# Splitting half of the experts' weights one layer earlier, and taking the two products of an expert tile in turns

## The chip, the cores and the metric

The program runs on one core of a Trainium2 chip. The metric is device microseconds of one execution, median of several runs; the times here are of that one core, and the profile is of one further execution of the same program. PE is TensorE (PEld its weight loads), DVE VectorE, ACT ScalarE, POOL GpSimd, SP the sync engine that only issues DMAs.

## What is computed

A two-layer network on 4096 tokens of width 256 (128 sequences of 32), with a context of 257 rows for each sequence. Layer 0 is softmax cross-attention, a state space block and a quantized feed-forward block; layer 1 is cut out here, with what the change touches:

```python
x = x + _L1_xattn_ref(_layernorm(x, axis=-1), ctx_1024, ctx_1024, L1_xattn_Wq, L1_xattn_Wk, L1_xattn_Wv, L1_xattn_Wo)  # sigmoid
x = x + _L1_attn_ref(_layernorm(x, axis=-1), L1_attn_w_qkv, L1_attn_w_proj, L1_attn_b_proj)                            # softmax
x = x + _L1_ffn_ref(_layernorm(x, axis=-1), L1_ffn_switch_w, L1_ffn_switch_b, L1_ffn_w1, L1_ffn_b1, L1_ffn_w2, L1_ffn_b2)
...
logits = t @ switch_w + switch_b
route_prob = jax.nn.softmax(logits, axis=-1)
route_prob_max = jnp.max(route_prob, axis=-1)
routes = jnp.argmax(route_prob, axis=-1)
for e in range(n_experts):                     # 8 experts, 256 -> 1024 -> 256
    h = jax.nn.gelu(t @ w1[e] + b1[e])
    y = h @ w2[e] + b2[e]
    mask = (routes == e)[:, None]
    out = jnp.where(mask, y, out)
out = out * route_prob_max[:, None]
```

Each token goes through one expert of eight.

## The kernel before

Every float32 factor is kept as two float16 halves, a high and a low one, and a product of two factors is three products on PE (high by high, high by low, low by high). The work is written out by hand: each engine has its own list of instructions in a fixed order, and counts in semaphores tie the lists together. An engine that waits holds up everything behind it in its list. Each layer is a block with a barrier at its end.

**Experts' weights.** There are 16 pieces (two per expert) of 128 by 2048 numbers, split into halves in the tile `ea_w` (`Ahead.W`). Splitting a piece is: SP loads it, ACT writes the high half (`hi_w`, a scaled copy), DVE or POOL writes the low half (`lo_w`, the staged number minus the high half). Pieces 0 to 7 are split in self-attention, a quarter of a piece in each of its 32 steps: `hi_w` (L2458) stands last in ACT's step and `lo_w` (L2569) last in DVE's, just ahead of `add_max` of the step after the next. Pieces 8 to 15 are split in `sort_tokens`, which finds each token's expert: DVE takes four of them in the loop over 32 token tiles, POOL four behind it. The space of pieces 8 to 15 is lent to tiles of self-attention (`lent`) until then.

**Sigmoid cross-attention** (`x_` names, L934) runs over 128 sequences in 32 groups of four. In a sequence PE computes scores, keys of the sequence after the next, one of three small jobs for the next group (`turn`), `attend` of the sequence before the last, and values of the next one. DVE's list for the second sequence of a group (j = 1) ends with `lo_q`; behind it come, for j = 2, `extract` (L1398, `x_oT`) and `lo_v` (L1391, `x_vl`). PE's `attend` (L1219) waits for that `extract`, and PE's next `values` (L1105, `x_psV`) for that `lo_v`. POOL's `spread` (L1066) starts when `lo_q` is done.

**Self-attention** (`a_` names, L2131) has 32 steps of 128 tokens. DVE's step is: `add_max` of the next step, `lo_pT` (L2550), a few more, `extract` (L2559), `lo_ob`, `lo_q` or `lo_v`, `count`, `lo_w`. PE's `attend` waits for `lo_pT`, ACT's and DVE's `extract` for `attend`.

**Expert tiles** (`e1t_` names, L2899). 39 tiles of up to 128 tokens of one expert. For a tile, PE transposes the normalised rows (L2950), then `hidden`: 8 blocks k of four products with 256, 128, 256, 128 columns (L2966, L2967), then `outputs` of the tile before: 8 pairs with 512 and 256 columns (L2978, L2979). The expert's number is only known at run time, so the address of a weight comes from a register: an instruction that works it out stands ahead of each hidden product and of each pair of output products, and `value_load` reads the number behind the transposes. Between the tiles this chain runs:

```python
act.wait_ge(h_mm, s * 2 + (half + 1))             # take_low, L3016: PE's last hidden product of tile s
dve.wait_ge(low_taken, s * 2 + (half + 1))        # add_bias, L3115
dve.wait_ge(row_in[c], i * 16 + 16)               # normalise(s + 2), L3099, behind add_bias in DVE's list
pe.wait_ge(xn_done, s + 1)                        # transpose(s), L2950, ahead of value_load and hidden in PE's list
```

so `transpose(s + 2)`, which PE's list has at the start of tile s + 1, waits for the last hidden product of tile s by way of ACT and DVE.

Of the kernel before, what the change touches and what calls it, by code (L numbers as in the profile page):

```python
# [18 lines left out]
P = 128  # L19
D = 256  # L20
# [913 lines left out]
def sigmoid_attention(nc, d, xres, con, norm):  # L934
# [4 lines left out]
    with ExitStack() as ctx:  # L939
# [10 lines left out]
        ctxp = parts("ctx", [P, GB, C, LAST], 2)  # L950
# [4 lines left out]
        vxr = [sb(f"vxr{n}", [64, GB, D], F16) for n in range(2)]  # L955
        vxm = [sb(f"vxm{n}", [64, GB, D], F16) for n in range(2)]
# [56 lines left out]

        @block.sync
        def _(sync):
# [29 lines left out]
            run(sync, body)  # L1045

# [207 lines left out]
        def _(act):  # L1254
# [50 lines left out]

            def hi_ob(i, gp):
# [17 lines left out]
            def body(i):  # L1324
                for c in range(8):
# [15 lines left out]
            hi_ob(LASTI, 1)  # L1341

        @block.vector
        def _(dve):
# [36 lines left out]
            def lo_k(i, c):  # L1381
# [3 lines left out]
                dve.tensor_tensor(flat(K[c % 4][1]), psK[:], flat(K[c % 4][0]), ALU.subtract).then_inc(k_lo, 1)  # L1385

# [39 lines left out]
            def body(i):  # L1426
                for c in range(8):
# [19 lines left out]
            residual(LASTI, 1)  # L1447

# [682 lines left out]
def self_attention(nc, d, xres, con, norm, ahead):  # L2131
# [10 lines left out]
    with ExitStack() as ctx:  # L2142
# [10 lines left out]
        late = ahead.W[:, AHEAD:].rearrange("p n h f -> p (n h f)")  # L2153
        free = [0]

        def lent(dims, turns, axes):

            size, pairs = math.prod(dims.values()), []
            for _ in range(turns):
                pairs.append(tuple(late[:, free[0] + n * size:free[0] + (n + 1) * size].rearrange(axes, **dims) for n in range(2)))  # L2160
                free[0] += 2 * size
            return pairs
# [24 lines left out]
        w_in, w_hi, w_lo = sem("w_in"), sem("w_hi"), sem("w_lo")  # L2187
        stage = sb("stage", [P, PIECE], F32)
# [216 lines left out]
        def _(act):  # L2405
# [72 lines left out]
            def body(i):  # L2478
                for c in range(2 * U):
# [16 lines left out]
                    hi_w(i, c)  # L2496
# [3 lines left out]
        def _(dve):  # L2500
# [68 lines left out]
            def lo_w(i, c):  # L2569
                g = i * 2 * U + c  # L2570
                dve.wait_ge(w_hi, g + 1)
                dve.scalar_tensor_tensor(ahead.W[:, g // 4, 1, quarter(g)], stage[:, quarter(g)], WS,
                                         ahead.W[:, g // 4, 0, quarter(g)], ALU.mult, ALU.subtract).then_inc(w_lo, 1)

# [20 lines left out]
            def body(i):  # L2595
                for c in range(2 * U):
# [19 lines left out]
                    lo_w(i, c)  # L2616
# [7 lines left out]

class Ahead:
# [3 lines left out]
    def __init__(self, nc, sp, d):  # L2629
        self.W = sp.sb("w", [P, 16, 2, PIECE], F16)  # L2630
# [637 lines left out]
```

## Time and profile before

| | |
|---|---|
| median of 3 runs | 2903.12 us (2901.89 to 2906.99) |
| the profiled execution | 2901.02 us |
| its span | 2899.2 us, mean granted clock 0.928 |
| PE busy | 2486.8 us (86%) |
| DVE busy | 2180.6 us (75%) |
| ACT busy | 1935.3 us (67%) |
| POOL busy | 1614.3 us (56%) |

The span is from the first to the last instruction; the execution's own time has 1.8 us around it. The busy time is a sum over stages with different limits. By the starts of their first instructions the stages that the change touches are the sigmoid cross-attention (about 1480 to 2106 us), self-attention (to 2494), the sort (to 2591) and the expert tiles (to the end). The granted clock is PE's, as a share of 2.4 GHz.

### The profile page before, as it was taken

Reading aid. Unit: us, or ns where it says so; the run is one execution under the profiler, and the core shown is the slowest. Engines: PE = TensorE matmul, PEld = TensorE weight load, DVE = VectorE, ACT = ScalarE, POOL = GpSimd, SP = SyncE. Lnnn points to the kernel's source line nnn. Section 1 sums busy time; section 2 is a strip of 40 time slices with the busy share of each in tenths; the row PEclk is TensorE's granted clock in tenths of the full one; section 3 lists DMA queues with packets and bytes.
Section 4 is the critical chain, followed back from the end, with each engine's and each line's share of the span. In section 5 each row is a group of like instructions: output and inputs, shape, how many; then the busy total and the mean of one; then the engine's idle time right before and its main releaser. Section 6 shows DMA issues by size and latency. Waiting matters only on the chain. (4 is left out here: it accounts for less than half of the span.)

```text
span 2899.2 us, 97754 instructions
## 1 busy us (share of the span) xinstructions
PE 2486.8 (86%) x38790; PEld 1920.0 (66%) x38790; DVE 2180.6 (75%) x4939; ACT 1935.3 (67%) x4320; POOL 1614.3 (56%) x1709
## 2 busy tenths in 40 slices
PE   3999999999928999976969999999947777639997
PEld 2777777777715777753548888888736666526665
DVE  4899999999947999974367777777658888456665
ACT  2788888888838999943447777777735555335554
POOL 3776777777534555520056766666436566435554
PEclk9999999999958999997989999999969889559999
DMA  5222222222100000000022221222011111221110
GB/s 155 64 75 70 70 71 83 70 70 71 31 15 1 1 1 1 1 15 17 1 86 68 68 63 57 68 68 68 19 36 35 37 43 44 84 65 36 38 38 29
DMA packets 123292, 140.20 MB, mean 48 GB/s; under 512 B 17184, under 2 KB 115264, under 8 KB 120672
## 3 DMA queue, kind: packets, MB, share of 16 engines
q1 hardware_dynamic: 114992, 123.60, 14.2%
q0 software_dynamic: 3744, 10.31, 1.2%
q8 instruction: 316, 5.18, 0.8%
q14 instruction: 128, 1.05, 0.1%
q10 hardware_dynamic: 4112, 0.07, 0.1%
HBM read 123.78 MB, written 10.16 MB: 46 GB/s over the span
## 5 line engine op out<-in xcount | busy, mean ns | idle before, releaser
L2081 DVE TENSOR_TENSOR_SCAN m_s<-m_a,m_psBx 128x2048 f32<-128x2048 f32 x64 | 282.7, 4417 | 21.6 <-PE m_psBx L1856 18.8
L1377 DVE SCALAR_TENSOR_TENSOR x_pTl<-x_psS,x_pTh 128x1024 f16<-128x1024 f32 x128 | 156.7, 1224 | 174.1 <-ACT x_pTh L1285 174.1
L676 ACT ACTIVATE x_prob<-x_prob,x_low 128x257 f32<-128x257 f32 x512 | 254.4, 513 | 5.2 <-DVE x_low L802 3.5
L1867 PE MATMUL m_psS<-m_s,all_ident 128*128 128x256 f32 x1024 | 237.3, 385 | 0.9 <-DVE m_s L2081 0.9
L1867 PEld LDWEIGHTS m_psS<-m_s,all_ident 128*128 128x128 f32 x1024 | 190.2, 191 | 42.8 <-issue 18.2
L802 DVE CUSTOM_DVE_ANT_0 x_prob<-x_psS,x_masked,x_prob 128x256 f32<-128x256 f32 x512 | 216.1, 477 | 1.6 <-PE x_psS L558 1.4
L1988 ACT ACTIVATE m_a<-m_dt,m_rate 128x248 f32<-128x248 f32 x512 | 205.8, 489 | 5.0 <-DVE m_s L2081 4.6
L691 ACT ACTIVATE x_kh<-x_psK,x_bk 128x256 f16<-128x256 f32 x256 | 107.3, 470 | 131.7 <-PE x_psK L442 131.7
L817 DVE SCALAR_TENSOR_TENSOR x_pTl<-x_psT,x_pTh 128x512 f16<-128x512 f32 x256 | 163.4, 679 | 0.5 <-ACT x_pTh L684 0.5
L2966 PE MATMUL e1t_psH<-e1t_xnp,ea_w 128*128 128x256 f16 x624 | 159.8, 284 | 2.3 <-issue 0.5
L1066 POOL TENSOR_TENSOR x_qbdh<-x_qh,all_mask4h 128x1024 f16<-128x1024 f16 x32 | 60.6, 1893 | 181.6 <-DVE x_ql L1358 181.6
L2290 PE MATMUL a_psO<-ea_w 128*64 128x128 f16 x1536 | 98.5, 264 | 71.8 <-DVE ea_w L2550 71.8
L2235 POOL TENSOR_TENSOR ea_w<-ea_w,all_mask4h 128x1024 f16<-128x1024 f16 x64 | 121.3, 1899 | 61.5 <-DVE ea_w L2511 61.5
L1058 POOL TENSOR_TENSOR x_ctxl<-x_ctx,x_ctxh 128x512 f16<-128x512 f32 x128 | 149.4, 1167 | 10.6
L1298 ACT ACTIVATE x_vh<-x_psV 128x512 f16<-128x512 f32 x128 | 76.4, 597 | 116.8 <-PE x_psV L1105 116.8
L347 POOL TENSOR_TENSOR x_ctxl<-x_ctx,x_ctxh 128x512 f16<-128x512 f32 x128 | 148.4, 1159 | 10.7
L442 PE MATMUL x_psK<-x_ctxh,x_wkh 128*128 128x256 f16 x512 | 141.2, 276 | 6.2 <-POOL x_ctxl L347 5.0
L2290 PEld LDWEIGHTS a_psO<-ea_w 128*64 128x64 f16 x1536 | 92.6, 138 | 80.8 <-DVE ea_w L2550 80.8
L1279 ACT ACTIVATE x_psS<-x_psS 128x1024 f32<-128x1024 f32 x128 | 129.0, 1008 | 24.3 <-PE x_psS L1199 24.3
L1105 PE MATMUL x_psK<-x_ctxh,x_wkh 128*128 128x256 f16 x512 | 141.2, 276 | 3.9 <-POOL x_ctxl L1058 3.6
L3060 POOL TENSOR_TENSOR e1t_hidl<-e1t_g,e1t_hidh 128x512 f16<-128x512 f32 x78 | 93.0, 1192 | 92.3 <-ACT e1t_hidh L3032 89.6
L3115 DVE SCALAR_TENSOR_TENSOR all_xres<-e1t_psH,e1t_bias,all_xres 128x128 f32<-128x128 f32 x312 | 87.9, 344 | 74.2 <-ACT all_xres L3016 37.4
(552 smaller groups left out, 10071.3 us busy)
## 6 DMA issues: line engine op xcount, KB each, us to landing
x_ctx<-in_ctxT SPq DMA_DIRECT2D x64, 1024.0 KB, 6.1
x_mraw<-in_mask SPq DMA_DIRECT2D x128, 128.5 KB, 2.8
a_stage<-in_L_ffn_w SPq DMA_DIRECT2D x8, 1024.0 KB, 5.0
e1r_stage<-in_L_ffn_w SPq DMA_DIRECT2D x8, 1024.0 KB, 5.1
all_xres<-in_x SPq DMA_DIRECT2D x1, 4096.0 KB, 14.5
x_vxr<-x_vx SPq DMA_DIRECT2D x128, 32.0 KB, 3.6
e_x<-all_xres SPq DMA_DIRECT2D x32, 128.0 KB, 2.0
x_vxr<-x_vx SPq DMA_DIRECT2D x96, 8.0 KB, 2.3
```

The lines of the kernel that those rows point to most:

```text
L347: pool.tensor_tensor(lo[:, j], src, hi[:, j], ALU.subtract).then_inc(ctx_split, 1)
L442: last = pe.matmul(out, a, b, start=m == 0, stop=m == len(prods) - 1)
L676: act.activation(prob[c % 4][:, h, :], prob[c % 4][:, h, :], ACT.Exp, bias=low[c % 4][:, h:h + 1], scale=-1.0, accum_out=sm[c % 2][:, h:h ...
L802: dve.tensor_tensor_reduce(prob[c % 4][:, h, 0:LAST], psS[:, to:to + LAST], masked[gp][:, j, 0:LAST], -SC, prob[c % 4][:, h, LAST:S2], ALU ...
L817: dve.scalar_tensor_tensor(turned(pT[c % 2][1], r), strip_of(psT, r), PS, turned(pT[c % 2][0], r), ALU.mult, ALU.subtract).then_inc(pt_lo, 1)
L1058: pool.tensor_tensor(lo[:, j], src, hi[:, j], ALU.subtract).then_inc(ctx_split, 1)
L1377: dve.scalar_tensor_tensor(pT[c % 4][1][:].rearrange("p r k n -> p (r k n)"), psS[c % 2][:], PS, pT[c % 4][0][:].rearrange("p r k n -> p ( ...
L1867: last = pe.matmul(psS[:, h * ST:(h + 1) * ST], con["ident"][:], S[h][:, :, m, :], start=m == 0, stop=m == NS - 1)
L1988: last = act.activation(A[h][:, :, m, 1:T], dt[c % 2][:, h, :].rearrange("p (b t) -> p b t", t=T)[:, :, 1:T], ACT.Exp, scale=rate[:, h, m: ...
L2081: dve.tensor_tensor_scan(rows(S), rows(A), psBx[:], 0.0, ALU.mult, ALU.add).then_inc(scan_done, 1)
L2290: last = pe.matmul(out, a, b, start=m == 0, stop=m == len(prods) - 1)
L2966: pe.matmul(at, wh, x[:, :, cc, :], start=cc == 0, stop=False)
```

## The change

1. The loads, `hi_w` and `lo_w` of pieces 0 to 7 move from self-attention into the sigmoid cross-attention: one quarter piece per group of four sequences, `hi_w` behind ACT's list for j = 3, `lo_w` behind DVE's list for j = 1, two staging buffers of a quarter instead of one of a whole piece. To make room, larger tiles of that layer (`ctx`, `vxr`, `vxm`, `qbd`, K, V, `pT`) live in the space of pieces 8 to 15 (`Lent`), so the weights' tile exists from that layer on and is called `ew_w`.
2. In `sort_tokens` the transposed tiles have three buffers instead of two, PE transposes two tiles ahead, DVE writes three low halves (pieces 0, 2 and 4 of the eight) and POOL five: two in the loop over tiles and three behind it. The last two high halves on ACT stand ahead of the copy that waits for DVE's `tile_ready`.
3. In the expert tiles, PE takes the 8 blocks of `hidden` of tile s and the 8 pairs of `outputs` of tile s - 2 in turns; outputs lie one tile further back, and `hid` has three buffers.

```diff
 # sigmoid_attention
+            def load_w(q):
+                wait(sync, w_lo, q - 1)
+                sync.dma_start(stage[q % 2][:], d["L1_ffn_w"][q // 4][:, quarter(q)]).then_inc(w_in[q % 2], 16)
 ...
                     load_vx(i, gp)
+                    if i * 2 + gp:
+                        load_w(i * 2 + gp - 1)
 ...
+            def hi_w(q):
+                act.wait_ge(w_in[q % 2], (q // 2 + 1) * 16)
+                act.activation(experts_w[:, q // 4, 0, quarter(q)], stage[q % 2][:], ACT.Copy, scale=WS).then_inc(w_hi, 1)
 ...
+                    if j == 3 and i * 2 + c // 4:
+                        hi_w(i * 2 + c // 4 - 1)
 ...
+            def lo_w(q):
+                dve.wait_ge(w_hi, q + 1)
+                dve.scalar_tensor_tensor(experts_w[:, q // 4, 1, quarter(q)], stage[q % 2][:], WS,
+                                         experts_w[:, q // 4, 0, quarter(q)], ALU.mult, ALU.subtract).then_inc(w_lo, 1)
 ...
+                    if j == 1 and i * 2 + c // 4 > 1:
+                        lo_w(i * 2 + c // 4 - 2)
             run(dve, body)
 ...
             residual(LASTI, 1)
+            lo_w(NT - 2)
+            lo_w(NT - 1)
 # self_attention
-                    hi_w(i, c)
 ...
                     if exists(i, c, -1):
                         count(i, c)
-                    lo_w(i, c)
             run(dve, body)
 # sort_tokens
-    LATE, BY_POOL = 16 - AHEAD, 4
+    LATE = 16 - AHEAD
+    BY_DVE = {0: 1, 2: 2, 4: 3}
+    BY_POOL = {1: 1, 3: 2, 5: 3, 6: 4, 7: 5}
 ...
             transpose(0)
+            transpose(1)
             for t in range(NT):
-                if t + 1 < NT:
-                    transpose(t + 1)
+                if t + 2 < NT:
+                    transpose(t + 2)
                 logits(t)
 ...
-            scale_w(LATE - BY_POOL)
+            for k in (6, 7):
+                scale_w(k)
+                hi_w(k)
             act.wait_ge(tile_ready, 1)
             act.activation(named[:, :, 1, :], oh_tile, ACT.Copy, scale=row[:]).then_inc(row_ready, 1)
-            for k in range(LATE - BY_POOL + 1, LATE):
-                scale_w(k)
 ...
-            for k in range(LATE - BY_POOL, LATE):
-                hi, lo = halves(k)
-                pool.wait_ge(w_hi, k + 1)
-                pool.tensor_tensor(lo, stage[k % 2][:], hi, ALU.subtract).then_inc(w_lo_pool, 1)
-            pool.wait_ge(w_lo_pool, BY_POOL)
+                if t in (13, 23):
+                    lo_w((t - 8) // 5)
+            for k in (5, 6, 7):
+                lo_w(k)
+            pool.wait_ge(w_lo_pool, len(BY_POOL))
 # expert_tiles, PE
-                    if exists(i, c, 1):
-                        transpose(*at(i, c, 1))
-                        e[s + 1] = expert(pe, *at(i, c, 1))
-                    if exists(i, c, 0):
-                        hidden(i, c, e[s])
-                    if exists(i, c, -1):
-                        outputs(*at(i, c, -1), e.pop(s - 1))
-            run(pe, body)
+            for s in range(SLOTS + 2):
+                if s + 1 < SLOTS:
+                    transpose(s + 1)
+                    e[s + 1] = expert(pe, s + 1)
+                for k in range(FC):
+                    if s < SLOTS:
+                        hidden(s, e[s], k)
+                    if s >= 2:
+                        outputs(s - 2, e[s - 2], k)
+                e.pop(s - 2, None)
 # expert_tiles, DVE: the order is kept, and finish lies one tile further back
-                    if exists(i, c, -1):
-                        finish(*at(i, c, -1))
+                if s >= 2:
+                    finish(s - 2)
```

PE's list in the middle of the expert tiles, before: the last hidden product of a tile, the eight pairs of output products (the first and the last shown), the transposes, the expert's number (TENSOR_LOAD), and the first product of the next tile. ISA rows are the register instructions.

```order
L2967 MATMUL e1t_psH<-e1t_xnp,ea_w 128x128
L2978 ISA
L2978 MATMUL e1t_psY<-ea_w,e1t_hidh 128x512
L2979 MATMUL e1t_psY<-ea_w,e1t_hidl 128x256
...
L2950 MATMUL e1t_psX<-all_ident,e1t_xn 128x128 x2
L2941 TENSOR_LOAD e_owner
L2941 ISA x2
L2966 ISA
L2966 MATMUL e1t_psH<-e1t_xnp,ea_w 128x256
```

The same place now (the names are the same but for `ew_w`; lines are those of the changed kernel): the last block of hidden products, one pair of output products, the transposes.

```order
L2977 MATMUL e1t_psH<-e1t_xnp,ew_w 128x256
L2978 ISA
L2978 MATMUL e1t_psH<-e1t_xnp,ew_w 128x128
L2987 ISA
L2987 MATMUL e1t_psY<-ew_w,e1t_hidh 128x512
L2988 MATMUL e1t_psY<-ew_w,e1t_hidl 128x256
L2965 MATMUL e1t_psX<-all_ident,e1t_xn 128x128 x2
L2954 TENSOR_LOAD e_owner
L2954 ISA x2
L2977 ISA
L2977 MATMUL e1t_psH<-e1t_xnp,ew_w 128x256
```

Between the last hidden product and the transposes there were eight pairs of output products; now there is one, and the other seven stand among the hidden products.

DVE's list in the sigmoid cross-attention, from j = 1 into j = 2, before:

```order
L1385 TENSOR_TENSOR x_kl<-x_psK,x_kh 128x512
L1358 TENSOR_TENSOR x_ql<-x_psM,x_qh 128x256
L1361 TENSOR_TENSOR x_qx<-x_psM,x_kx 128x128 x2
L1398 SCALAR_TENSOR_TENSOR x_oT<-x_psO,all_mask,x_oT 128x2x64
L1391 TENSOR_TENSOR x_vl<-x_psV,x_vh 128x512
L1377 SCALAR_TENSOR_TENSOR x_pTl<-x_psS,x_pTh 128x1024
```

And now, with tiles of the layer inside `ew_w`:

```order
L1405 TENSOR_TENSOR ew_w<-x_psK,ew_w 128x512
L1378 TENSOR_TENSOR x_ql<-x_psM,x_qh 128x256
L1381 TENSOR_TENSOR x_qx<-x_psM,x_kx 128x128 x2
L1409 SCALAR_TENSOR_TENSOR ew_w<-x_stage,ew_w 128x512
L1423 SCALAR_TENSOR_TENSOR x_oT<-x_psO,all_mask,x_oT 128x2x64
L1416 TENSOR_TENSOR ew_w<-x_psV,ew_w 128x512
L1397 SCALAR_TENSOR_TENSOR ew_w<-x_psS,ew_w 128x1024
```

`lo_w` (L1409) has come between the last work of j = 1 and `extract` and `lo_v` of j = 2.

## Rows read from the trace of the kernel before

**Rows 1.** Windows: us, busy of PE, PEld, DVE, ACT, POOL, granted clock, DMA

```profile
1480.00:2095.00 615.00, 611.02 (x13114) 498.28 (x13115) 428.86 (x692) 457.74 (x728) 410.73 (x351) 0.99 0.21 61
2165.00:2485.00 320.00, 240.11 (x3776) 202.92 (x3775) 258.69 (x479) 178.84 (x327) 191.48 (x149) 0.89 0.11 37
2605.00:2880.00 275.00, 271.92 (x1883) 180.19 (x1884) 168.41 (x484) 153.79 (x303) 161.32 (x148) 1.00 0.12 36
```

**Rows 2.** Chain that ended last: output products of tiles 2 and 35

```profile
2624.06 0.39 PE e1t_psY L2978
...
2866.64 0.39 PE e1t_psY L2978
```

**Rows 3.** Timeline, PE, tiles 4 and 5: start, duration, what

```profile
2631.18 0.23 PE L2967 MATMUL e1t_psH<-e1t_xnp,ea_w 128*128 128x128 f16 x1
2631.43 0.39 PE L2978 MATMUL e1t_psY<-ea_w,e1t_hidh 128*128 x1
...
2634.04 0.38 PE L2950 MATMUL e1t_psX<-all_ident,e1t_xn 128*128 128x128 f32 x2
2634.45 0.28 PE L2966 MATMUL e1t_psH<-e1t_xnp,ea_w 128*128 128x256 f16 x1
2634.57 0.23 PE L2967 MATMUL e1t_psH<-e1t_xnp,ea_w 128*128 128x128 f16 x1
```

**Rows 4.** Timeline, ACT and DVE, end of the same tile 4

```profile
2631.45 0.60 ACT L3016 ACTIVATE all_xres<-e1t_psH 128x512 f32<-128x512 f32 x1 [1.59 <-PE e1t_psH L2967]
...
2633.12 0.41 DVE L3099 TENSOR_SCALAR e1t_xn<-e1t_row 128x256 f32<-128x256 f32 x1
```

**Rows 5.** Timeline of PE, tiles 0 and 1, then a window there

```profile
2600.87 0.22 PE L2967 MATMUL e1t_psH<-e1t_xnp,ea_w 128*128 128x128 f16 x1
2600.93 0.27 PE L2966 MATMUL e1t_psH<-e1t_xnp,ea_w 128*128 128x256 f16 x1
2601.03 0.22 PE L2967 MATMUL e1t_psH<-e1t_xnp,ea_w 128*128 128x128 f16 x1
...
2604.19 0.69 PE L2950 MATMUL e1t_psX<-all_ident,e1t_xn 128*128 128x128 f32 x2 [2.17 <-DVE e1t_xn L3099]
...
2604.10:2607.40 3.30, 3.03 (x17) 2.16 (x18) 0.46 (x2) 2.75 (x6) 2.04 (x2) 0.50 0.00 0
```

**Rows 6.** Self-attention, DVE and POOL: timeline, then the line, then its group

```profile
2318.33 1.89 POOL L2235 TENSOR_TENSOR ea_w<-ea_w,all_mask4h 128x1024 f16<-128x1024 f16 x1 [3.34 <-DVE ea_w L2511]
...
2318.50 2.27 DVE L2572 SCALAR_TENSOR_TENSOR ea_w<-a_stage,ea_w 128x512 f16<-128x512 f32 x1
2320.69 0.41 DVE L2533 SCALAR_TENSOR_TENSOR a_prob<-a_psS,all_phi 128x256 f32<-128x256 f32 x1
...
L2572 DVE SCALAR_TENSOR_TENSOR ea_w<-a_stage,ea_w x32: 666/676/2271, 2171.0 to 2492.3; 128x512 f16<-128x512 f32 x32
...
L2572 DVE SCALAR_TENSOR_TENSOR ea_w<-a_stage,ea_w 128x512 f16<-128x512 f32 x32 | 42.3, 1321 | 0.0
```

**Rows 7.** Sigmoid cross-attention, timeline of POOL, DVE and PE in one group

```profile
1806.29 1.89 POOL L1066 TENSOR_TENSOR x_qbdh<-x_qh,all_mask4h 128x1024 f16<-128x1024 f16 x1 [5.94 <-DVE x_ql L1358]
...
1806.53 0.34 DVE L1398 SCALAR_TENSOR_TENSOR x_oT<-x_psO,all_mask,x_oT 128x128 f32<-128x128 f32 x1
1806.78 0.68 DVE L1391 TENSOR_TENSOR x_vl<-x_psV,x_vh 128x512 f16<-128x512 f32 x1
...
1808.78 0.21 PE L1219 MATMUL x_psO<-x_pTh,x_vh 128*32 128x64 f16 x4
...
1809.42 0.28 PE L1105 MATMUL x_psV<-x_wvh,x_ctxh 128*128 128x256 f16 x1
```

**Rows 8.** Timeline of DVE and POOL, end of the sort

```profile
2582.10 0.18 DVE L2896 CAST e_token<-e1r_own 128x39 uint32<-128x39 f32 x1
...
2586.05 4.05 POOL L2799 TENSOR_TENSOR ea_w<-e1r_stage,ea_w 128x2048 f16<-128x2048 f32 x1 [5.05 <-ACT ea_w L2767]
2591.67 1.19 POOL L3066 DMA_INDIRECT e1t_row<-e_x,e_token  x1 [1.57 <-SPq L2904]
```

More of the change, by code:

```diff
@@ L1341, in _ @@
             hi_ob(LASTI, 1)
+            hi_w(NT - 1)
         @block.vector
@@ L2151, in parts @@
             return [(sb(f"{name}h{n}", shape, F16), sb(f"{name}l{n}", shape, F16)) for n in range(turns)]
[L2153 to L2162, printed above, removed]
+        lent = Lent(ahead.W)
         xn = sb("xn", [P, 2, D], F32)
@@ L2622, with __init__, __call__ @@
 PIECE, AHEAD = C * 8 * P, 8
+class Lent:
+    def __init__(self, experts_w):
+        self.late, self.used = experts_w[:, AHEAD:].rearrange("p n h f -> p (n h f)"), 0
+    def __call__(self, dims, turns, axes, rows=P):
+        size, pairs = math.prod(dims.values()), []
+        for _ in range(turns):
+            pairs.append([self.late[0:rows, self.used + n * size:self.used + (n + 1) * size].rearrange(axes, **dims) for n in range(2)])
+            self.used += 2 * size
+        return pairs
 class Ahead:
-    def __init__(self, nc, sp, d):
-        self.W = sp.sb("w", [P, 16, 2, PIECE], F16)
+    def __init__(self, nc, sp, d, experts_w):
+        self.W = experts_w
         self.x_dram = nc.dram_tensor("e1_x", (TOK + P, D + 4), F32, kind="Internal").ap()
@@ L2756, in _ @@
         def _(act):
-            def hi_w(k):
-                hi, _ = halves(k)
-                act.wait_ge(w_in[k % 2], (k // 2 + 1) * 16)
-                act.activation(hi, stage[k % 2][:], ACT.Copy, scale=WS).then_inc(w_hi, 1)
             def scale_w(k):
@@ L3050, in _ @@
-            run(act, body)
+                    wait(act, y_mm, s - 2)
+                act.activation(hid[s % 3][0][:, four(half), :], g[s % 2][:, four(half), :], ACT.Copy).then_inc(hid_hi, 1)
+            hi_xn(0)
+            take_bias(0)
+            for s in range(SLOTS):
+                if s + 1 < SLOTS:
+                    hi_xn(s + 1)
+                take_low(s, 0)
+                take_low(s, 1)
+                for half in range(2):
+                    gelu(s, half)
+                    hi_hid(s, half)
+                if s + 1 < SLOTS:
+                    take_bias(s + 1)
@@ L3089, in _, with gather, lo_hid @@
-            run(pool, body)
+            def gather(s):
+                wait(pool, o_done, s - U + 1)
+                pool.indirect_dma_start(row[s % U][:], None, x_dram, bass.IndirectOffsetOnAxis(ap=token[:, s:s + 1], axis=0))\
+                    .then_inc(row_in[s % U], 16)
+            def lo_hid(s, half):
+                pool.wait_ge(hid_hi, s * 2 + (half + 1))
+                if half == 0:
+                    wait(pool, y_mm, s - 2)
+                pool.tensor_tensor(hid[s % 3][1][:, four(half), :], g[s % 2][:, four(half), :], hid[s % 3][0][:, four(half), :],
+                                   ALU.subtract).then_inc(hid_lo, 1)
@@ new lines, in scatter @@
+            def scatter(s):
+                pool.wait_ge(o_done, s + 1)
+                wait(pool, put[(s - 1) % U], ((s - 1) // U + 1) * 16)
+                pool.indirect_dma_start(out, bass.IndirectOffsetOnAxis(ap=token[:, s:s + 1], axis=0), o[s % 4], None)\
+                    .then_inc(put[s % U], 16)
+            for s in range(EARLY):
+                gather(s)
+            for s in range(SLOTS + 2):
+                if s + EARLY < SLOTS:
+                    gather(s + EARLY)
+                if s < SLOTS:
+                    lo_hid(s, 0)
+                    lo_hid(s, 1)
+                if s >= 2:
+                    scatter(s - 2)
```

329 lines of the change are left out of this document (129 added, 200 removed).

## The prediction, made before the changed kernel ran

> **What bounds the kernel now.** I read the stages first, each for the wait that ends last in it. In the sigmoid cross-attention PE is busy 611 of 615 us and DVE 429: PE sets the pace, and only a delay of PE costs [rows 1]. In self-attention PE is busy 240 of 320 us, DVE 259, and the granted clock is 0.89: no engine is full, a loop through several engines is the limit [rows 1]. Its closed part is DVE's `lo_pT`, PE's `attend`, ACT's and DVE's `extract`, the rest of DVE's step, `lo_w`, `add_max`, and `lo_pT` again, so DVE time just ahead of `add_max` is on the path. In the expert tiles PE is busy 272 of 275 us at clock 1.00 [rows 1], which looks like a PE bound. It is not one. The output products of tiles 2 and 35 start at 2624.06 and 2866.64 us, so a tile takes 242.58 / 33 = 7.35 us [rows 2]. Inside it, the last hidden product of tile 4 starts at 2631.18 and the first of tile 5 at 2634.45, 3.27 us later, with the eight pairs of output products and the transposes between them [rows 3]. The same distance without any output products stands between tiles 0 and 1: the chain's transposes start at 2604.19 after 2.17 us of idle PE, released by DVE's normalising [rows 5]. In tile 4 that chain shows as ACT at 2631.45 and DVE's normalising at 2633.12 to 2633.53, while the transposes are held by the output products to 2634.04 [rows 3, 4]. So the 3.27 us are the chain PE, ACT, DVE, transposes, reading the expert's number, and the outputs (2631.43 to 2634.04, 2.6 us) lie in its shadow and are free. The other 7.35 - 3.27 = 4.08 us are 31 steps from one hidden product to the next, 0.13 us each, whether 256 or 128 columns (0.12 in the rows) [rows 3]. Where products had queued up while the array was slow, they go 0.06 and 0.10 us apart [rows 5]; so 0.13 us is the time of the instruction stream with its address instructions, and PE does buffer issued products.
>
> **Expert tiles: the sum.** In turns, a block is five address instructions, 5 x 0.13 = 0.65 us of issue, and at the array two times (0.10 + 0.06) plus a pair of outputs. Eight pairs take 2.6 us, so one takes 0.33, and the array needs 0.65 us [rows 3, 5]. Since PE buffers, a block takes the larger, 0.66 us; without buffering 4 x 0.13 + 0.33 = 0.85. From the first to the last hidden product of a tile that is 7 x 0.66 + 3 x 0.13 = 5.0 us, with 0.1 for the first block, where nothing is queued yet. The chain behind it is untouched by the edit: the same waits, and DVE still normalises tile s + 2 only behind the biases of tile s. So a tile takes 3.27 + 5.1 = 8.37 us. Only the last pair of outputs (0.33 us) is left in the shadow of the chain. Tiles 2 to 37 have both products and the chain, 36 x (8.37 - 7.35) = +37 us at full clock.
>
> Then the clock. PE now idles about 3.27 - 0.33 - 0.13 - 0.4 = 2.4 us in every tile, some 1.9 of it in one piece. The only tile that had such a gap, 2.17 us, was followed by a stretch at 0.50, 2604.1 to 2607.4 us [rows 5], that is 1.2 GHz. Self-attention, with PE three quarters busy and its idle time in one piece per step too, is granted 0.89 [rows 1]. In the new body a block is bound by the array as much as by issue, so a stretch of 3.3 us at half level does 3.3 / 1.31 = 2.5 blocks instead of 5 and costs 1.65 us. Never gives 8.37 us, in every tile 10.0. I take three tiles in four, 9.6 us: 36 x 2.25 = **+81 us**, bounds +37 and +96.
>
> The Trainium skill ("TensorE: Matmul & The Clock Gate", section "Why this matters for your kernels") asks only that PE not idle longer than what is idle here in one piece. By that rule the clock stays up and the stage costs +37. The row of tile 1 speaks against it.
>
> **Self-attention: -50 us.** The 32 `lo_w` leave DVE. They take 42.3 us, median 0.676, up to 2.271 [rows 6]. The long ones start while POOL's `spread` runs: 2318.50 against 2318.33 to 2320.22, and `add_max` follows at 2320.69, 2.19 us after [rows 6]. A short one holds the next up by 0.68 - 0.09 = 0.59 us. (42.3 - 32 x 0.676) / (2.27 - 0.676) = 13 are long: 13 x 2.19 + 19 x 0.59 = 39.7 us, all ahead of `add_max`, thus on the loop. What is late next is `attend`, which still waits for `lo_pT`: PE has 320 - 240 = 80 us of idle time, 2.5 us a step, so even 2.19 fits. `hi_w` on ACT is covered by ACT's waits (busy 179 of 320 us) and is taken at nothing, 0.5 us a step at most if not. Denser PE work also gives clock back: at 0.89, 22% of 320 us are at half level, 70 us; half the speed in the third or so of a step in which `attend` sets the pace is 12 us; I take 10. Bounds -36 (some of it kept by POOL) and -56.
>
> **Sigmoid cross-attention: +14 us.** 32 `hi_w` and `lo_w` arrive. ACT has 157 us free and PE does not wait for what is behind `hi_w`. `lo_w` is another matter: it stands right behind `lo_q`, which is what starts POOL's `spread`, 1806.29 to 1808.18. It would start at about 1806.53, be held to 1808.2 and end at 1808.75 [rows 7]. Behind it `extract` (now 1806.53, 0.34 us) would end at 1809.0 and `lo_v` (now 1806.78, 0.68 us) at 1809.65. PE's `attend` at 1808.78 waits for the one, `values` at 1809.42 for the other [rows 7]: both about 0.3 us late, and 0.1 more for `lo_k` behind them. 0.4 x 31 groups = 12.4 us, and the two last `lo_w` behind the layer's last `residual` add 1.3. Bounds: 0, since the slack is known to 0.3 us only, and 2.2 us a group, 68, if all of it reached PE.
>
> The Trainium skill ("SBUF — State Buffer", section "Who interferes with whom") says the port pair shared by VectorE and GpSimd is an exclusive lock for a whole instruction. Rows 6 agree for `lo_w`, 2.27 us against 0.68. If POOL kept the pair through both instructions of `spread`, each `lo_w` would be held 1.9 us more, and the layer would come near the upper bound.
>
> **Sort: -8 us.** The token numbers are ready at 2582.3, but POOL's last low half runs from 2586.05 to 2590.1 and the first gather starts at 2591.67 [rows 8]. Now the last high halves are ahead of the copy that waits for DVE, and POOL is through with 6 and 7 before 2570. The 7.8 us go. One POOL low half (4.05 us) moves into DVE's serial part and two into the loop, while the ones that overlapped DVE's end leave: I take these as even, bounds -18 and 0.
>
> **Sum**, against the profiled execution: 2901.0 + 81 - 50 + 14 - 8 = 2938 us. The profiled execution is 2.1 us below the median of the runs shown, less than I can tell; I leave it at 2938.
>
> **Rivals.**
> 1. The clock stays up in the tiles: +37 instead of +81, 2894 us, faster by 0.3%. For it: the clock is 1.00 in all tiles with a gap under a microsecond. Against it: tile 1. The step decides at 3 half-level stretches in 10 tiles. Chance 0.17.
> 2. `lo_w` in the cross-attention reaches PE in full: 68 instead of 14, 2992 us. For it: PE has no slack there. Against it: rows 7 leave 1.9 of 2.2 us before PE asks. Chance 0.07.
> 3. The chain is hidden after all, and PE runs at 8 x 0.66 + 0.4 = 5.7 us a tile: 36 x (5.7 - 7.35) = -59, 2798 us. For it: products that don't wait are ready while PE waits. Against it: PE's list is taken in order, and the transposes stand ahead of all of them. Chance 0.04.
> 4. The forecast, 0.72: its own range is 2912 to 2965 (the bounds of the clock in the tiles, and some 10 us for the other stages).
>
> **How the numbers follow.** 0.2%, about what a measurement of this kernel can tell, is 5.8 us. Of the forecast's 0.72 I give 0.70 to slower, rival 2 adds 0.07, rival 1 splits into 0.03 slower, 0.04 same and 0.10 faster, rival 3 is faster. Slower 0.79, same 0.06, faster 0.15. The range leaves out rivals 2 and 3 and takes in most of 1: 2892 to 2966.
>
> **What would show it.** Right: in the tiles the transposes start 2.4 us after the last hidden product, with PE idle; a tile takes over 8.3 us; stretches at 0.50 in most; the step of self-attention falls from 10.3 to about 8.8 us; `lo_w` in the cross-attention lasts about 2.2 us, and a group grows by 0.4. Wrong: a granted clock of 1.00 through the tiles, blocks of 0.85 us, or a tile below 7.35 us.

## The result, and the profile of the changed kernel

The changed kernel takes 2947.41 us (2945.67 to 2949.07, 4 runs) where the kernel before took 2905.05 in the same runs: ratio 1.0147, 95% interval 1.0129 to 1.0164: slower by 1.5%. The forecast was 2938, its range 2892 to 2966. The profiled execution has a span of 2944.2 us against 2899.2. By stage these 45.0 us are as follows. The stages are cut at PE's first product of the cross-attention, the end of DVE's last instruction there and in self-attention, and the start of POOL's first gather:

| stage | before | changed | difference | forecast |
|---|---|---|---|---|
| all ahead of the cross-attention | 1474.9 | 1472.2 | -2.6 | 0 |
| sigmoid cross-attention | 631.4 | 647.2 | +15.8 | +14 |
| self-attention (with its opening) | 388.3 | 340.1 | -48.1 | -50 |
| sort, to the first gather | 97.2 | 81.8 | -15.4 | -8 |
| expert tiles | 307.5 | 402.8 | +95.3 | +81 |

The -2.6 us lies in layers that the change doesn't touch.

**Windows** of the changed kernel (us, busy of PE, PEld, DVE, ACT, POOL, granted clock, DMA), the same three stages as in [rows 1], then two stretches inside the tiles:

```profile
1480.00:2105.00 625.00, 609.60 (x13051) 495.91 (x13049) 479.23 (x721) 473.43 (x758) 422.99 (x348) 1.00 0.26 73
2165.00:2449.00 284.00, 226.18 (x3875) 188.82 (x3871) 228.76 (x459) 174.88 (x312) 197.78 (x154) 0.94 0.05 16
2560.00:2910.00 350.00, 267.14 (x1757) 173.39 (x1754) 149.30 (x460) 145.29 (x284) 154.31 (x139) 0.84 0.09 27
2702.80:2706.20 3.40, 3.40 (x16) 2.09 (x17) 0.41 (x1) 0.00 (x0) 2.75 (x3) 0.51 0.11 39
2706.20:2713.10 6.90, 4.60 (x37) 2.99 (x36) 4.05 (x13) 4.08 (x8) 1.93 (x2) 0.99 0.07 19
```

In the expert tiles PE's share fell from 99% to 76% and the clock from 1.00 to 0.84. The last two rows follow each other across one tile and the start of the next: 3.4 us at half level, then 6.9 at full.

**Timeline of PE**, that tile, in the changed kernel (start, duration, what, idle time before and what ended it):

```profile
2701.31 0.44 PE L2965 MATMUL e1t_psX<-all_ident,e1t_xn 128*128 128x128 f32 x2 [1.85 <-DVE e1t_xn L3086]
2702.17 0.28 PE L2977 MATMUL e1t_psH<-e1t_xnp,ew_w 128*128 128x256 f16 x1 [0.43 <-issue]
...
2704.03 0.63 PE L2987 MATMUL e1t_psY<-ew_w,e1t_hidh 128*128 x1
...
2705.31 0.63 PE L2987 MATMUL e1t_psY<-ew_w,e1t_hidh 128*128 x1
...
2707.74 0.38 PE L2987 MATMUL e1t_psY<-ew_w,e1t_hidh 128*128 x1
...
2708.39 0.38 PE L2987 MATMUL e1t_psY<-ew_w,e1t_hidh 128*128 x1
...
2708.99 0.22 PE L2978 MATMUL e1t_psH<-e1t_xnp,ew_w 128*128 128x128 f16 x1
2709.05 0.38 PE L2987 MATMUL e1t_psY<-ew_w,e1t_hidh 128*128 x1
...
2711.38 0.44 PE L2965 MATMUL e1t_psX<-all_ident,e1t_xn 128*128 128x128 f32 x2 [1.85 <-DVE e1t_xn L3086]
2712.24 0.28 PE L2977 MATMUL e1t_psH<-e1t_xnp,ew_w 128*128 128x256 f16 x1 [0.42 <-issue]
```

Read the distances. From the last hidden product (2708.99) to the first of the next tile (2712.24) are 3.25 us: the chain of [rows 3], unchanged, but now it holds 1.85 us of idle PE where the eight output pairs were. A block is 0.65 us at full clock (2707.74 to 2708.39) and 1.28 at half (2704.03 to 2705.31). A tile is 2712.24 - 2702.17 = 10.07 us. Over the 37 distances that the trace shows between the first hidden products of two tiles, a tile takes 9.82 us on average. The first two have no output products beside them (8.34 and 7.70 us). The other 35 take 9.92 us on average, and three of these, without a stretch at half level, take 8.45 to 8.47.

**Cross-attention**, POOL, DVE and PE at the place of [rows 7], then the line of the low half and of `lo_q` (x count, duration ns min/median/max, first and last start):

```profile
1809.52 1.90 POOL L1079 TENSOR_TENSOR ew_w<-x_qh,all_mask4h 128x1024 f16<-128x1024 f16 x1 [3.11 <-DVE x_ql L1378]
1811.37 2.34 POOL L1079 TENSOR_TENSOR ew_w<-x_ql,all_mask4h 128x1024 f16<-128x1024 f16 x1
...
1809.75 2.21 DVE L1409 SCALAR_TENSOR_TENSOR ew_w<-x_stage,ew_w 128x512 f16<-128x512 f32 x1
1811.88 0.34 DVE L1423 SCALAR_TENSOR_TENSOR x_oT<-x_psO,all_mask,x_oT 128x128 f32<-128x128 f32 x1
...
1812.44 0.55 PE L1232 MATMUL x_psO<-ew_w 128*32 128x64 f16 x48 [0.36 <-issue]
...
L1409 DVE SCALAR_TENSOR_TENSOR ew_w<-x_stage,ew_w x32: 682/2208/2209, 1533.2 to 2118.7; 128x512 f16<-128x512 f32 x32
L1378 DVE TENSOR_TENSOR x_ql<-x_psM,x_qh x32: 415/415/425, 1481.8 to 2085.0; 128x256 f16<-128x256 f32 x32
```

The low half runs while `spread` does and lasts 2.21 us; `attend` comes after 0.36 us of idle PE. The usual group (the median distance from one `lo_q` to the next of its kind) takes 19.61 us where it took 19.16.

**Self-attention and sort**: `add_max`'s second instruction of the changed kernel and of the one before (32 steps), then the last token number and the first gather of the changed kernel:

```profile
L2542 DVE TENSOR_REDUCE a_mx<-a_prob x32: 686/686/689, 2168.6 to 2441.0; 128x16 f32<-128x512 f32 x32
...
L2538 DVE TENSOR_REDUCE a_mx<-a_prob x32: 685/686/687, 2155.4 to 2475.9; 128x16 f32<-128x512 f32 x32
...
2539.58 0.18 DVE L2922 CAST e_token<-e1r_own 128x39 uint32<-128x39 f32 x1
2541.38 1.19 POOL L3051 DMA_INDIRECT e1t_row<-e_x,e_token  x1 [16.42 <-SPq L2931]
```

A step is (2441.0 - 2168.6) / 31 = 8.79 us, before 10.34. In the sort the gather starts 1.6 us behind the token numbers, no longer 9.4 [rows 8].

### The profile page after: what moved, and what is told of

The parts are those of the page before. It is cut to its first block and busy times, and to the rows that moved or that the text cites. A ratio compares the mean times of both kernels' runs of the same rounds, so it can differ in the third digit from the quotient of the medians.

```text
span 2944.2 us, 97775 instructions
## 1 busy us (share of the span) xinstructions
PE 2482.5 (84%) x38790; PEld 1909.7 (65%) x38790; DVE 2186.6 (74%) x4938; ACT 1941.3 (66%) x4321; POOL 1638.1 (56%) x1710
## 3 DMA queue, kind: packets, MB, share of 16 engines
q14 instruction: 128, 1.05, 0.1%
## 5 line engine op out<-in xcount | busy, mean ns | idle before, releaser
L1397 DVE SCALAR_TENSOR_TENSOR ew_w<-x_psS,ew_w 128x1024 f16<-128x1024 f32 x128 | 156.3, 1221 | 136.6 <-ACT ew_w L1298 136.6
L3058 POOL TENSOR_TENSOR e1t_hidl<-all_xres,e1t_hidh 128x512 f16<-128x512 f32 x78 | 96.3, 1234 | 198.6 <-ACT e1t_hidh L3032 195.9
L1118 PE MATMUL x_psV<-x_wvh,ew_w 128*128 128x256 f16 x1024 | 189.9, 274 | 0.0
L2977 PE MATMUL e1t_psH<-e1t_xnp,ew_w 128*128 128x256 f16 x624 | 168.4, 320 | 16.5 <-issue 16.4
L1118 PE MATMUL x_psK<-ew_w,x_wkh 128*128 128x256 f16 x1024 | 176.7, 274 | 3.5 <-POOL ew_w L1071 3.1
L1071 POOL TENSOR_TENSOR ew_w<-x_ctx,ew_w 128x512 f16<-128x512 f32 x128 | 149.6, 1169 | 10.7
L347 POOL TENSOR_TENSOR x_ctxl<-x_ctx,x_ctxh 128x512 f16<-128x512 f32 x128 | 148.9, 1163 | 10.7
L2245 POOL TENSOR_TENSOR ew_w<-ew_w,all_mask4h 128x1024 f16<-128x1024 f16 x64 | 121.0, 1895 | 59.1 <-DVE ew_w L2515 59.1
L442 PE MATMUL x_psK<-x_ctxh,x_wkh 128*128 128x256 f16 x512 | 141.9, 277 | 5.8 <-POOL x_ctxl L347 5.1
L2978 PE MATMUL e1t_psH<-e1t_xnp,ew_w 128*128 128x128 f16 x624 | 145.8, 250 | 0.0
```

The costliest lines, as they stand in the source:

```text
L347: pool.tensor_tensor(lo[:, j], src, hi[:, j], ALU.subtract).then_inc(ctx_split, 1)
L1071: pool.tensor_tensor(lo[:, j], src, hi[:, j], ALU.subtract).then_inc(ctx_split, 1)
L1118: last = pe.matmul(out, a, b, start=m == 0, stop=m == len(prods) - 1)
L1397: dve.scalar_tensor_tensor(pT[c % 4][1][:].rearrange("p r k n -> p (r k n)"), psS[c % 2][:], PS, pT[c % 4][0][:].rearrange("p r k n -> p ( ...
L2977: pe.matmul(at, wh, x[:, :, cc, :], start=cc == 0, stop=False)
L2978: last = pe.matmul(at[:, 0], wl, x[:, 0, cc, :], start=False, stop=cc == C - 1)
```

## Experiments

All are timed in turns with the kernel before; that measured 2907.6, 2908.0 and 2901.4 us in the three sets, and 2905.1 beside the changed kernel. So a difference between times of two sets is uncertain by 3 to 7 us, and where it matters the stages of the traces are compared.

**order_back: the products not in turns.**

```diff
                 for k in range(FC):
                     if s < SLOTS:
                         hidden(s, e[s], k)
+                for k in range(FC):
                     if s >= 2:
                         outputs(s - 2, e[s - 2], k)
```

> The changed kernel, but with all eight hidden blocks of tile s ahead of the eight output pairs of tile s - 2, not in turns. Theory (the outputs used to lie in the shadow of the chain hidden, ACT, DVE's biases, normalising, transposes, and taking them out of it is what costs): the period of a tile is 7.35 us again, the granted clock 1.00, and the stage is 95 us shorter than in the changed kernel: 2947 - 95 = 2852 us. Rival (the stage is slower for something else of its rewrite: outputs one tile further back, three hid buffers, an unrolled list): the period stays near 10 us, 2947 us.

2861.87 us (2860.05 to 2863.66), ratio 0.984 (0.9824 to 0.9857). A window in the tiles:

```profile
2600.00:2780.00 180.00, 172.45 (x1187) 113.09 (x1184) 113.38 (x308) 97.31 (x191) 103.52 (x95) 1.00 0.12 36
```

The clock in the tiles is 1.00 and a tile takes 7.60 us. The stage is 318.8 us, 84 less than in the changed kernel and 11 more than before: the turn-taking is nearly all of the loss. The rest (0.25 us a tile, and a turn more at the end) belongs to the other things that part 3 rewrites, outputs one tile further back and three `hid` buffers among them; no run separates these.

**tiles_only: the third part of the change alone,** in the kernel before; the function is replaced whole by that of the changed kernel.

```diff
-def expert_tiles(nc, xres, con, ahead, b2, owner, token, out):
-    SLOTS, PIECE, FC, U = owner.shape[1], 2048, 8, 8
...
+def expert_tiles(nc, xres, con, ahead, b2, owner, token, out):
+    SLOTS, FC, U, EARLY = owner.shape[1], 8, 8, 3
...
```

> The kernel before with only the third part of the change: the expert tiles of the changed kernel in place of its own. Theory (this part alone is the loss, and it does not depend on the others): the stage grows by 95 us as in the changed kernel, period 9.8 us, clock 0.84: +3.3%, 3000 us where before measures 2905. Rival (the stage suffers also from how the weights or the sort were left behind by parts 1 and 2): clearly less than 95 us, below 2985.

2994.71 us (2994.0 to 2996.3), ratio 1.0298 (1.0282 to 1.0313). A window in the tiles:

```profile
2600.00:2780.00 180.00, 136.33 (x906) 89.27 (x904) 76.50 (x238) 77.41 (x150) 78.20 (x71) 0.84 0.09 26
```

A tile takes 9.75 us at a clock of 0.84. The stage is 400.4 us, 93 more than before where the changed kernel has 95 more; the program is 87 us slower than the kernel before of its set. The loss belongs to this part and doesn't need the other two.

**filler: something for PE to do in the gap.** The 14 products are read by nobody.

```diff
                         outputs(s - 2, e[s - 2], k)
+                if s < SLOTS:
+                    for n in range(14):
+                        pe.matmul(psF[:, 0:2 * P].rearrange("p (a t) -> p a t", t=P), xnp[s % 2][:, 0, 0, :], xnp[s % 2][:, :, 1, :],
+                                  start=n == 0, stop=n == 13)
```

> The changed kernel with 14 products of 256 columns on a free PSUM bank behind the last output pair of every tile; their result is read by nothing. They fill 1.5 us of PE's idle time and the chain is left as it is. Theory (the idle time is what brings the clock down): granted clock 1.00 through the tiles, a tile takes 8.45 us, and 33 stretches at half level, 1.62 us each, are gone: 2947 - 53 = 2894 us. Rival (the clock falls for the denser products in turns, not for the idle time): the clock stays at 0.84 or falls further, the fillers take up to 3 us where it is at half level, and the tile gets longer: 2947 to 2985 us.

2894.96 us (2893.15 to 2895.78), ratio 0.9955 (0.9938 to 0.9972): 52 us less than the changed kernel, with 39 x 14 products more. Timeline of PE and a window of this run:

```profile
2686.24 1.69 PE L3006 MATMUL e1t_psF<-e1t_xnp 128*128 128x256 f16 x14
2688.25 0.44 PE L2966 MATMUL e1t_psX<-all_ident,e1t_xn 128*128 128x128 f32 x2 [0.32 <-DVE e1t_xn L3091]
2689.12 0.28 PE L2978 MATMUL e1t_psH<-e1t_xnp,ew_w 128*128 128x256 f16 x1 [0.43 <-issue]
...
2600.00:2780.00 180.00, 163.96 (x1357) 117.02 (x1356) 89.26 (x274) 85.90 (x169) 93.23 (x84) 1.00 0.11 33
```

Nothing in the chain is shorter (3.27 us on average), but the clock is 1.00 and a tile takes 8.45 us. So it was the idle time that brought the clock down, and the clock's share of the stage's loss is 9.82 - 8.45 = 1.37 us a tile, the rest the products taken out of the shadow.

**norm_first: normalising ahead of the biases** on DVE, in the changed kernel.

```diff
+                if s + 2 < SLOTS:
+                    normalise(s + 2)
                 if s < SLOTS:
                     add_bias(s, 0)
                     add_bias(s, 1)
-                if s + 2 < SLOTS:
-                    normalise(s + 2)
```

> The changed kernel with one line moved on DVE: normalise(s + 2) ahead of the biases of tile s, not behind them. Theory (the transposes wait for ACT and DVE only by DVE's order): PE no longer idles between tiles, the clock stays at 1.00, and a tile takes the body at full clock, 5.2 us, plus the last pair, the transposes and the expert's number, 0.33 + 0.13 + 0.41: 6.1 us, up to 6.4 if ACT or DVE (busy 4.1 and 4.5 us a tile) get in the way. 36 x (10.07 - 6.2) = 139 us less: 2808 us, 2800 to 2822. Rival (another link of the chain ends at nearly the same time, PE's wait for free psH or ACT's list): 8.4 us a tile, 2890 us. Rival (PE's own work is the bound): 2947 us.

2813.75 us (2812.27 to 2815.75), ratio 0.9678 (0.9662 to 0.9694). Timeline of PE and the window:

```profile
2702.61 0.38 PE L2965 MATMUL e1t_psX<-all_ident,e1t_xn 128*128 128x128 f32 x2
2703.30 0.28 PE L2977 MATMUL e1t_psH<-e1t_xnp,ew_w 128*128 128x256 f16 x1 [0.31 <-issue]
...
2708.88 0.38 PE L2965 MATMUL e1t_psX<-all_ident,e1t_xn 128*128 128x128 f32 x2
2709.75 0.28 PE L2977 MATMUL e1t_psH<-e1t_xnp,ew_w 128*128 128x256 f16 x1 [0.50 <-issue]
...
2600.00:2780.00 180.00, 169.10 (x1416) 119.17 (x1414) 128.10 (x372) 114.25 (x227) 120.83 (x113) 1.00 0.14 44
```

The transposes have no wait before them, a tile takes 6.3 us. The only thing that made them wait for ACT and DVE was an order in DVE's list; the data that normalising reads had been there.

**before_norm_first: the same line moved in the kernel before.**

```diff
+                        if exists(i, c, 2):
+                            normalise(*at(i, c, 2))
                         add_bias(i, c, 0)
                         add_bias(i, c, 1)
-                    if exists(i, c, 2):
-                        normalise(*at(i, c, 2))
```

> The kernel before with the same one line moved on DVE: normalising ahead of the biases. Theory (before, the chain is covered: the transposes are held by the output products until 2634.04 while normalising ends at 2633.53): nothing is gained, a tile takes 7.3 us, 2903 us within 6. Rival (the chain bounds the kernel before as well): a tile loses part of 3.27 us, at 1 us each 2866 us or less.

2860.17 us (2857.41 to 2860.36), ratio 0.9833 (0.9817 to 0.985): 47 us gained where my theory said none. A tile takes 6.30 us. Timeline of PE:

```profile
2703.43 0.38 PE L2978 MATMUL e1t_psY<-ea_w,e1t_hidh 128*128 x1
2703.65 0.27 PE L2979 MATMUL e1t_psY<-ea_w,e1t_hidl 128*128 x1
2703.76 0.38 PE L2950 MATMUL e1t_psX<-all_ident,e1t_xn 128*128 128x128 f32 x2
2703.98 0.27 PE L2966 MATMUL e1t_psH<-e1t_xnp,ea_w 128*128 128x256 f16 x1
2704.09 0.22 PE L2967 MATMUL e1t_psH<-e1t_xnp,ea_w 128*128 128x128 f16 x1
2704.14 0.27 PE L2966 MATMUL e1t_psH<-e1t_xnp,ea_w 128*128 128x256 f16 x1
...
2707.04 0.23 PE L2967 MATMUL e1t_psH<-e1t_xnp,ea_w 128*128 128x128 f16 x1
2707.17 0.28 PE L2966 MATMUL e1t_psH<-e1t_xnp,ea_w 128*128 128x256 f16 x1
2707.29 0.23 PE L2967 MATMUL e1t_psH<-e1t_xnp,ea_w 128*128 128x128 f16 x1
```

Compare the spacing. Early in the tile hidden products are 0.11 and 0.05 us apart, late in it 0.12 and 0.13. The early ones had been issued while the array still worked off the outputs. The 31 steps from the first hidden product to the last (2703.98 to 2707.29) take 3.31 us where they took 4.1 in the kernel before, and the first stands 0.22 us behind the transposes where it stood 0.41. In the kernel before PE's instruction stream stood at the transposes until 2633.5 us, half a microsecond short of the outputs' end [rows 3, 4], so nothing was queued. The wait cost no idle array at its place, and 1.05 us a tile later.

**no_run_ahead: that same kernel, with the instruction stream stopped again** by a wait for something that is not in the chain.

```diff
                     if exists(i, c, 1):
+                        wait(pe, y_mm, s - 1)
                         transpose(*at(i, c, 1))
```

> The run with normalising moved ahead in the kernel before gained 47 us where nothing was expected, and its trace shows hidden products 0.05 and 0.11 us apart after the outputs: products that were issued while the array was busy. Here the same kernel gets one wait more on PE: the transposes wait for the output products of the turn before. Theory (what the chain cost before was that PE's instruction stream stood still at the transposes until the outputs were nearly through, so that nothing was queued behind them): with this wait it stands still again, a tile takes 4.1 + 0.25 + 2.6 + 0.2 + 0.86 = 8.0 us, some 24 us more than before, 2930 us. Rival (the chain itself bounded the tile, since normalising ended too late for the transposes): the wait costs next to nothing, 6.3 us a tile, 2860 us.

2924.03 us (2921.07 to 2926.24), ratio 1.0054 (1.0039 to 1.0069). A tile takes 7.97 us:

```profile
2640.99 0.27 PE L2979 MATMUL e1t_psY<-ea_w,e1t_hidl 128*128 x1
2641.32 0.44 PE L2950 MATMUL e1t_psX<-all_ident,e1t_xn 128*128 128x128 f32 x2
2642.18 0.28 PE L2966 MATMUL e1t_psH<-e1t_xnp,ea_w 128*128 128x256 f16 x1 [0.43 <-issue]
```

The transposes are hardly later behind the outputs (0.33 us against 0.11), yet the tile is 1.67 us longer. Products that are queued early are what the moved line bought.

**low_half_early: the cross-attention's low half where DVE waits.**

```diff
                     lo_v(i, c)
+                    if j == 0 and i * 2 + c // 4 > 1:
+                        lo_w(i * 2 + c // 4 - 2)
                     lo_pT(i, c)
...
-                    if j == 1 and i * 2 + c // 4 > 1:
-                        lo_w(i * 2 + c // 4 - 2)
```

> The changed kernel with the low half of a quarter piece, in the sigmoid cross-attention, put behind the low half of V of the first sequence of a group, where DVE then waits 1.56 us for ACT, not at the end of the second sequence, where POOL's spread holds it. Theory (PE waits 0.45 us a group for what stands behind a low half of 2.2 us): the low half takes 0.7 us, the group 19.16 us again as before, 31 x 0.45 = 14 us less: 2933 us. Rival (a group is longer for something else that came in: ACT's high half or the loads of a quarter): 19.6 us a group and 2947 us. Half of it if POOL's next low half, held for 0.3 us, reaches PE's keys.

2929.51 us (2926.89 to 2931.31), ratio 1.0071 (1.0057 to 1.0084); the span is 15.7 us shorter than the changed kernel's. The lines of the low half and of `lo_q`:

```profile
L1409 DVE SCALAR_TENSOR_TENSOR ew_w<-x_stage,ew_w x32: 681/866/869, 1526.7 to 2103.5; 128x512 f16<-128x512 f32 x32
...
L1378 DVE TENSOR_TENSOR x_ql<-x_psM,x_qh x32: 415/415/425, 1483.6 to 2070.8; 128x256 f16<-128x256 f32 x32
```

0.87 us instead of 2.21, and 587.2 us from the first `lo_q` to the last where the changed kernel took 603.2. The usual group is 19.16 us again. ACT's high half and the quarter loads cost nothing.

**attention_again: DVE's time put back into self-attention,** on data of its own; nothing reads it.

```diff
                     if exists(i, c, -1):
                         count(i, c)
+                    dve.wait_ge(again_in, i * 2 * U + c + 2)
+                    dve.scalar_tensor_tensor(again16[:], again[:], WS, again16[:], ALU.mult, ALU.subtract).then_inc(again_in, 1)
```

> The changed kernel with one extra instruction in every self-attention step of DVE, of the same form as the low half that was taken out there (128x512 float32 with a float16 operand to float16), at the same place, on data of its own that nothing reads. ACT's high half and the load are not put back. Theory (the whole gain of the stage, 48 us, is DVE's time ahead of add_max, with half of the instructions held by POOL's spread): the stage is 369 us again, 48 us more than the changed kernel: 2995 us. Rival (a good part of the gain came from ACT's high half or the weights' DMA): 10 to 30 us more.

2996.16 us (2993.62 to 2999.31), ratio 1.0303 (1.0287 to 1.0318), 49 us more than the changed kernel.

```profile
L2619 DVE SCALAR_TENSOR_TENSOR a_again<-a_again x32: 668/676/2273, 2182.8 to 2507.2; 128x512 f16<-128x512 f32 x32
L2543 DVE TENSOR_REDUCE a_mx<-a_prob x32: 686/686/687, 2168.1 to 2490.7; 128x16 f32<-128x512 f32 x32
```

Median and longest duration are those of [rows 6], and the step (322.6 / 31 = 10.41 us) is that of the kernel before, 10.34, within 0.1: the whole gain was DVE's time ahead of `add_max`, with what clock came with it, and none of it was ACT's or the loads'.

**act_order: ACT's late high halves ahead of its wait,** in the kernel before.

```diff
-            scale_w(LATE - BY_POOL)
+            for k in range(LATE - BY_POOL, LATE):
+                scale_w(k)
             act.wait_ge(tile_ready, 1)
             act.activation(named[:, :, 1, :], oh_tile, ACT.Copy, scale=row[:]).then_inc(row_ready, 1)
-            for k in range(LATE - BY_POOL + 1, LATE):
-                scale_w(k)
```

> The kernel before with one edit in the sort: ACT scales and writes the high halves of pieces 4 to 7 all ahead of the copy that waits for DVE's tile_ready. Theory (the 7.8 us that POOL's last low half ran behind the token numbers go with ACT's order alone; the other 7.5 us that the stage lost in the changed kernel come from the loop over tiles, 3.9 us, and from DVE instructions that POOL held at the end, 3.7 us): the gather starts 1.5 us behind the token numbers, not 9.4, 2898 us where before measures 2906. Rival (POOL's low halves are late for their loads or for their 4.05 us each, whatever ACT does): within 2 us of before. More than 8 us less if DVE's instructions at the end are no longer held either.

2896.4 us (2894.51 to 2899.82) against 2901.38, ratio 0.9986 (0.9977 to 0.9995): 4 to 5 us, about half of what was expected. The gather does start 1.6 us behind the end of the token numbers (2587.25, 2585.65), but these are 3.4 us later, since now DVE works beside all of POOL's late halves:

```profile
2568.22 10.49 POOL L2798 TENSOR_TENSOR ea_w<-e1r_stage,ea_w 128x2048 f16<-128x2048 f32 x2 [4.76 <-ACT ea_w L2767]
...
2569.58 5.21 DVE L2877 TENSOR_TENSOR all_xres<-all_xres,ea_tile 128x1248 f16<-128x1248 f16 x1
2574.94 8.12 DVE L2881 TENSOR_TENSOR all_xres<-ea_place_in,e1r_m 128x2048 f16<-128x2048 f32 x2
```

The second row took 1.46 us and the third 4.49 in the kernel before. In the changed kernel they take 1.46 and 4.49 us again: there two of POOL's five low halves went into the loop, and POOL is through before DVE gets to these two (2524.96 and 2531.07 us).

**best and parts_joined: the gains together.** The first is the changed kernel with the edits of norm_first and low_half_early, the second the same, with the expert tiles of before_norm_first.

```diff
+                if s + 2 < SLOTS:
+                    normalise(s + 2)
                 if s < SLOTS:
                     add_bias(s, 0)
...
                     lo_v(i, c)
+                    if j == 0 and i * 2 + c // 4 > 1:
+                        lo_w(i * 2 + c // 4 - 2)
```

> The changed kernel with both edits that helped: normalising ahead of the biases and the cross-attention's low half where DVE is idle. They lie in different stages, so the gains add: 2813.8 - 17.9 = 2796 us. Rival (they share something): above 2801.

> The same, but with the expert tiles of the kernel before (hidden, then outputs of the tile before, two hid buffers), normalising moved ahead there too. Theory (with products queued, PE's array sets a tile's 6.3 us and the order of its products is worth nothing; what is left is one turn less at the end, about 5 us): 2791 us. Rival (products in turns are better once the chain is hidden): the run in turns is faster by 1% or more.

best: 2798.69 us (2796.47 to 2799.66), ratio 0.9646 (0.9631 to 0.9661). parts_joined: 2794.68 us (2793.96 to 2796.79), ratio 0.9633 (0.9618 to 0.9647). By the times alone the gains add within 3 and 4 us. By the ratios they do not (low_half_early took 22 us off the changed kernel, and here only some 9 off norm_first), because the kernel before measured 6.6 us less in this set. The traces decide: the first gather starts 15.5 us earlier in low_half_early than in the changed kernel, and 13.7 us earlier in best than in norm_first. With the chain out of the way a tile takes 6.29 us with its products in turns and 6.32 without: the order of the products is worth nothing, and the 4 us between the two lie in the turn more at the end (from the first hidden product of tile 37 to the end of the span: 32.4 and 28.6 us).

## Why the prediction came out

**Tiles, +95.3 instead of +81.** The mechanism held at every step: the chain stayed 3.25 us, the outputs went onto the path (a block 0.65 us, forecast 0.66; a tile 8.45 us at full clock, forecast 8.37), PE idled 1.85 us in one piece (forecast 1.9), and a half-level stretch added 10.07 - 8.45 = 1.62 us (forecast 1.65). The term that was mis-sized is "I take three tiles in four": 32 of 35 tiles had a stretch, and the tiles with both kinds of products took 9.92 us on average, not 9.6. That is 36 x 0.32 = 11.5 us of the 14, 3 of them from the 0.08 us of the tile at full clock. The rest lies at the ends of the stage, where I left out the turn more that outputs two tiles back need; best and parts_joined differ by 4 us for it. The rule by which the clock would have stayed up (the Trainium skill, "TensorE: Matmul & The Clock Gate", section "Why this matters for your kernels") did not hold here: idle pieces of 1.85 us, shorter than the gap it warns of, took the clock to 0.84, and filling them brought back 1.00.

**What I had half wrong** is the sentence that the outputs are free in the chain's shadow and that the 3.27 us are fixed. They were free at the array. But the chain held PE's instruction stream in front of the transposes, and PE buffers what is issued, as I used in the sum for the new kernel; I did not ask what that buffer was worth in the old one. before_norm_first put 1.05 us a tile on it, and no_run_ahead took it away again.

**Self-attention, -48.1 instead of -50.** Right with its reason: a step fell from 10.34 to 8.79 us, and attention_again gave the time back. The granted clock rose from 0.89 to 0.94; the 10 us that I took for it I did not measure apart from the 40 us of DVE's time, so only their sum is confirmed.

**Cross-attention, +15.8 instead of +14.** `lo_w` took 2.21 us (forecast 2.2) and a group grew by 0.45 (forecast 0.4). The first instruction of `spread` ended at 1811.42, the low half at 1811.96, and the second instruction of `spread`, which started at 1811.37, took 2.34 us where it took 1.89 in the kernel before. So DVE got its turn between POOL's two instructions and POOL waited for it, and the upper bound did not come. This agrees with the Trainium skill ("SBUF — State Buffer", section "Who interferes with whom"), by which the lock is for one instruction.

**Sort, -15.4 instead of -8.** The 7.8 us of POOL's tail went as forecast. The step that failed is "I take these as even". By the traces the loop became 3.9 us shorter (from DVE's first normalising to its first `e1r_lg`: 45.9 and 42.0 us), and DVE's part behind it 3.7 us, since two DVE instructions that ran beside a low half of POOL's became one. The first two rows are the kernel before, the last is the changed one; an instruction of such a form takes 0.17 to 0.18 us without POOL beside it.

```profile
2573.26 3.77 DVE L2888 TENSOR_SCALAR e1r_own<-e1r_own 128x39 f32<-128x39 f32 x1
2577.07 3.98 DVE L2889 CAST e_owner<-e1r_own 128x39 int32<-128x39 f32 x1
...
2521.14 3.84 DVE L2881 TENSOR_SCALAR e1r_cnt<-e1r_inc 128x8 f32<-128x8 f32 x1
```

**The sum.** The spans differ by 45.0 us where the forecast had 37. Part of that nearness is luck: the tiles came out 14 us above their term and the sort 7 below it, and 2.6 us lie in layers that no term covers. Two of the chances are also added up wrongly: the shares named give 0.80 to slower and 0.14 to faster, not 0.79 and 0.15.

Of the rivals, the clock staying up is refuted by the window at 0.84, `lo_w` reaching PE in full by the group of 19.61, and the hidden chain by the 1.85 us of idle PE in each tile; norm_first shows what it takes to get that one.

**Open:** why a few of the tiles (some three of 35) escaped the half level, and how the 6.3 us of a tile without the chain divide: PE is 94% busy in norm_first and 99% in before_norm_first, and I tested no bound there.

## What to carry to other kernels

Before work is moved out of a gap, ask what ends the gap. If it is a chain through other engines, the gap stays, and all that filled it is added to the path; first break the chain, here by one line in DVE's list whose data had long been there. And a wait on a buffered engine can cost more than the idle time it shows: what counts is how far its instruction stream gets ahead while the array is still busy. Idle time on PE has a second price in the clock, so that here a gap of 1.85 us cost 1.62 us more in 32 of 35 tiles.

## What the hardware showed that I had not expected

- Useless products made the program faster: 14 in each tile, 1.69 us of array time, took it from 2947 to 2895 us, by way of the clock alone.
- Products of 256 and 128 columns with an address instruction ahead of each go 0.12 to 0.13 us apart when nothing is queued, and 0.11 and 0.05 apart when they had been issued ahead, in the same tile of the same kernel.
- Beside two POOL instructions of 128x2048 that follow each other, a DVE instruction that alone takes 1.46 us took 5.21; POOL's own went from 4.05 to up to 5.27 us each (act_order). Both sides lost.
